# Where GpSimd pauses between indirect transfers: a pause after every second one in four more places of a graph-network kernel

## The reference

```
x = x + _L0_gnn_ref(_layernorm(x), edge_index, W, a)        # weighted sum of neighbours' rows, summed by source
x = x + _L0_ffn_ref(_layernorm(x)[None], ...)               # 32 experts, one per node, hidden size 64
x = x + _L1_gnn_ref(_layernorm(x), edge_attr_8, edge_attr_4, ...)  # messages from edge attributes
x = x + _L1_ffn_ref(_layernorm(x)[None], ...)               # 6 experts, two per node, three layers of 256
x = x + _L2_gnn_ref(_layernorm(x), src, dst, ...)           # attention over edges, then a dense FFN
x = x + _L2_ffn_ref(_layernorm(x)[None], ...)               # dense mixture
x = x + _L3_gnn_ref(_layernorm(x), W, att, src, dst)        # attention over edges
x = x + _L3_ffn_ref(_layernorm(x)[None], ...)               # 8 experts, two per node
```

```
h = x @ W
e = exp(-leaky_relu((h @ a1)[src] + (h @ a2)[dst]))
h' = segment_sum(e * h[dst], src) / segment_sum(e, src)
```

## Time and profile before

| | us |
|---|---|
| median of 3 runs | 5369.42 (5359.68 to 5380.3) |
| the profiled execution | 5363.28 |
| its span in the profile | 5361.2 |
| first loop, first to last gather | 302.4 to 1030.1 |
| first FFN's slots, last SRT scatter to last result | 1217.7 to 1455.6 |
| two-expert slots | 2468 to 2648 and 5153 to 5322 |

### The profile page before, as it was taken

The page is one execution under the profiler, slowest core; times in us unless marked ns, Lnnn a source line. Parts: engine busy times, 40 slices in busy tenths (PEclk is TensorE's granted clock), DMA queues, the critical chain, the costliest instruction groups (busy, mean ns, idle before and its releaser), DMA issues.

```text
span 5361.2 us, 75037 instructions
## 1 busy us (share of the span) xinstructions
PE 3835.8 (72%) x19152; PEld 2523.5 (47%) x19152; DVE 3230.3 (60%) x8314; ACT 2680.6 (50%) x8902; POOL 2678.8 (50%) x3199
## 2 busy tenths in 40 slices
PE   6868888631529999987666776668999935556665
PEld 2336565431314444456545555545655524444454
DVE  9955666350337998876567788753333435555743
ACT  6835666420217888863336666653233325555522
POOL 4655555647357776704427777731000056666244
PEclk9978988755758999998888888889999967677778
DMA  3023322321313333422345555530000033333334
GB/s 121 21 73 82 80 78 78 59 51 36 106 46 89 90 89 86 87 41 93 105 129 160 160 161 161 159 85 0 12 12 16 6 93 86 86 84 85 34 118 131
DMA packets 278825, 441.41 MB, mean 82 GB/s; under 512 B 114083, under 2 KB 192781, under 8 KB 278157
## 3 DMA queue, kind: packets, MB, share of 16 engines
q0 software_dynamic: 124624, 331.70, 24.1%
q1 hardware_dynamic: 147230, 98.37, 6.4%
q10 hardware_dynamic: 6560, 6.55, 0.4%
HBM read 368.84 MB, written 67.60 MB: 81 GB/s over the span
## 4 chain that ended last, share of the span: by engine, by line
PE 40%; DVE 18%; another core or an unknown queue 12%; issue 12%; ACT 6%; POOL 6%; DMA 4%; DVEq 2%; ACTq 0%; POOLq 0%; SPq 0%
PE PB L3159 6%; PE PB L2012 5%; PE PB L2542 3%; PE PB L3143 3%; POOL bigt L2660 3%; PE PB L735 3%; PE PB L1092 2%; DVE bigt L714 2%; PE PB L1587 2%; ACT XNT L2626 2%; PE PB L1575 2%; PE PB L2022 2%; DMA bigt<-KVTAB,DO 2%; POOL X L2660 1%
## 5 line engine op out<-in xcount | busy, mean ns | idle before, releaser
L2542 PE MATMUL PB<-XNT 128*128 128x260 f32 x1760 | 598.5, 474 | 115.8 <-issue 46.0
L2660 POOL DMA_INDIRECT bigt<-ZTAB,DO x440 | 456.5, 1037 | 274.8 <-issue 120.8
L1036 POOL DMA_INDIRECT bigt<-HTAB,bigt x440 | 420.9, 957 | 314.1 <-ACT bigt L726 154.4
L1984 POOL DMA_INDIRECT bigt<-YTAB,bigt x440 | 473.5, 1076 | 140.3 <-issue 128.1
L366 POOL DMA_INDIRECT RECS<-bigt x391 | 388.4, 993 | 241.7 <-DVE bigt L714 96.0
L735 PE MATMUL PB<-bigt 128*128 128x440 f16 x1564 | 395.5, 382 | 89.5 <-issue 63.0
L2542 PEld LDWEIGHTS PB<-XNT 128*128 128x128 f32 x1760 | 366.1, 230 | 193.0 <-issue 66.4
L2626 ACT ACTIVATE XNT<-bigt 128x65 f32<-128x65 f32 x1768 | 446.2, 336 | 0.0
L726 ACT ACTIVATE bigt<-bigt 128x128 f16<-128x128 f16 x1214 | 374.3, 389 | 78.6 <-DVE bigt L699 41.6
L2012 PE MATMUL PB<-bigt 128*128 128x512 f32 x880 | 405.3, 603 | 3.0 <-DVE bigt L2200 3.0
L2660 POOL DMA_INDIRECT bigt<-KVTAB,DO x296 | 294.9, 996 | 214.5 <-DMA KVTAB<-bigt 83.5
(11 more groups left out here) (491 smaller groups left out, 9549.0 us busy)
## 6 DMA issues: line engine op xcount, KB each, us to landing
bigt<-YTAB,bigt POOLq DMA_INDIRECT x552
bigt<-SRT SPq DMA_DIRECT2D x56, 128.0 KB
OUTS<-bigt SPq DMA_DIRECT2D x56, 128.0 KB
SRT<-bigt SPq DMA_DIRECT2D x11, 640.0 KB, 9.9
bigt<-HTAB,bigt POOLq DMA_INDIRECT x440
bigt<-ZTAB,DO POOLq DMA_INDIRECT x440
KVTAB<-bigt SPq DMA_DIRECT2D x25, 258.0 KB
YTAB<-bigt SPq DMA_DIRECT2D x10, 640.0 KB, 9.6
```

The costliest lines, as they stand in the source:

```text
L1036: e.indirect_dma_start(out=Gt[:, g % GB, j, :], out_offset=None, in_=HTAB, in_offset=bass.IndirectOffsetOnAxis(ap=SO[:, g * G + j:g * G + ...
L1984: e.indirect_dma_start(out=Gt[:, g % GB, j, :], out_offset=None, in_=YTAB, in_offset=bass.IndirectOffsetOnAxis(ap=SO[:, g * G + j:g * G + ...
L2542: m = e.matmul(self.PV[n % len(self.PV)], self.OH[:, g % 2, j, :], self.msg[:, g % 2, j, :], start=(k == 0), stop=(k == self.H - 1))
L2660: e.indirect_dma_start(out=dst[:, j, :], out_offset=None, in_=table, in_offset=bass.IndirectOffsetOnAxis(ap=DO[:, g * G + j:g * G + j + 1] ...
```

## The change

- In the first loop the extra wait of a group's second pair (for `lanes_made` or `oht_kept`) is gone, and `rest(e)` stands after each pair of gathers.
- `attr_scatters` with n > 1 rests after every second scatter in place of every fourth. The calls with n = 1 (the first sort) have none, as before.
- The second batch of scatters in the first FFN has 30 in place of 36. The six are issued later: 65 in place of 59 are left for the second graph layer.
- The 25 SRT scatters rest after every second one.
- In the two-expert FFNs GpSimd rests once in each round of slots.

The calls of `rest` go from 279 to 698, that is 558 memsets to 1396. No instruction of another engine changes.

```
-                if (c - first) % 4 == 3:
+                if n > 1 and c % 2:
                     rest(e)
...
                         if g >= GB and j % 2 == 0:
                             e.wait_ge(*half(weighed, 2 * (g - GB) + j // 2))
-                            c = MOVES * (g - FIRST) + 1
-                            if j == 2 and 0 <= c < EC:
-                                e.wait_ge(*sort_d.lanes_made.at(sort_d.act_cols.index(c)))
-                            elif j == 2 and g - 3 < SG:
-                                e.wait_ge(*oht_kept.at(g - 3))
                         elif g >= 2 and j == 0:
                             e.wait_ge(*onehot.at(g - 2))
                         e.indirect_dma_start(
...
                         ).then_inc(gathered.sem(g), 16)
+                        if j % 2:
+                            rest(e)
...
                             ).then_inc(fetched.sem(s), 16)
+                        rest(e)
                     return
                 attr_scatters(e, 30)
                 e.wait_ge(*begun.last)
-                attr_scatters(e, 36)
+                attr_scatters(e, 30)
...
                         in_=xs[:, t, :], in_offset=None).then_inc(rows_out.sem, 16)
+                    if t % 2:
+                        rest(e)
                 attr_scatters(e, 116)
```

More of the change, by code:

```diff
@@ L354, in attr_scatters @@
         def attr_scatters(e, n):
-            first = recs_next[0]
-            for c in range(first, min(EC, first + n)):
+            for c in range(recs_next[0], min(EC, recs_next[0] + n)):
                 piece, k = divmod(c, PIECE)
@@ L1028, in pool_edges @@
                             e.wait_ge(*half(weighed, 2 * (g - GB) + j // 2))
[L1029 to L1033, removed]
                         elif g >= 2 and j == 0:
```

## The result

| | us |
|---|---|
| the changed kernel, median of 4 runs | 5230.01 (5220.94 to 5244.43) |
| the kernel before, same chip, 4 runs | 5371.21 (5359.68 to 5380.3) |
| ratio | 0.9741, 95% interval 0.9711 to 0.977 |
| the profiled execution; its span | 5244.43; 5242.7 |

The change makes the kernel faster by 141 us on this chip, where the forecast said 189 (5180); the time lies inside the range. A *stop* is here, as in the prediction, a stretch of a few us in which an engine waits for a signal that nothing in the profile claims ("remote"). The experiments add something that no profile of one chip could tell: **of the six chips that the experiments went to, two run the kernel before in 4850 us, the stops that the change removes are not there, and every set of its pauses that was run there costs time (the scatters' 34 us, the first loop's 139, the two-expert slots' 59 by the profiles).**

A forecast was written before the change was run, and what follows sets the result against it. Engines stand waiting for signals that come late while GpSimd issues indirect transfers without real pauses (12% unclaimed). Terms -63 -32 -10 +5 -68 -10 -11 sum to -189: 5363.3 to 5174, or 5180 by median; 8-in-10 range 5140 to 5345.

The forecast's parts named there:

- First loop, -63: First loop's 110 groups: stops go, GpSimd sets the pace, 727.7 us become 665; bounds -77 and 0.
- I take 0.45, by the nearer form: First loop: price of a pause in us, taken near the scatters' +0.43 and not the third graph layer's +0.74.
- Tail, -32: After the first loop's gathers, 61.9 us: without stops about 30 us; bounds 0 and -34.
- Routing -10, SRT +5: Routing, 67.8 us: stops go, -10; then 12 pauses among the SRT scatters stand on the path, +5.
- Slots, -68: First FFN's slots: all 56 results done within 172 us of scatters by twos, GpSimd's 76.9 us idle time gone.
- Second layer's start, -10: Second graph layer's start: 65 scatters by twos and a landing take 99.5 us against 109.6; bounds +15 and -12.
- Two-expert slots, -11: Second and last two-expert FFN: -8 and -3, pauses hidden while slots take over 3.0 us; bounds +10 and -25.
- The rest, 0: Second layer's loop, third and fourth graph layers, dense FFNs: same instructions, no change.
- The rival of half relief among scatters (5276): Pauses by two help only half as well among scatters as among gathers: sum -93, 5276; chance of half relief 0.26.
- The 5392 and 5452 of the slower rivals: Pauses that relieve nothing in loop or scatters, +29: 5392; dearer pauses, +89: 5452; chance of slower 0.15.
- GpSimd's pace takes the place of the stops, dearer than they are: First loop: pauses hold engines up instead of stops; at 0.95 us each the loop is +34, total 5452; slower 0.15.
- The rival of another cause: Stops come from something like code fetching, not GpSimd; loop unchanged: 5392 (slower 0.15) or 5375 (no change 0.07).

The follow-up runs named there:

- loop_alone_2: Kernel before with pauses after each pair of first-loop gathers and ScalarE's extra waits gone, on a chip with stops: 5306 us against 5367, ratio 0.989.
- no_slot_rest: Changed kernel without the pauses in the two-expert slots, on a chip with stops: 5209 us, ratio 0.9699 to the kernel before (5368).
- after_again: Changed kernel run once more, unchanged, on a chip with stops: 5226 us, ratio 0.974 to the kernel before (5368).
- waits_alone: Kernel before with ScalarE's extra first-loop waits gone and no pause put in, on a chip without stops: 4849 us against 4850, ratio 0.9997.
- loop_alone: Kernel before with pauses after each pair of first-loop gathers and ScalarE's extra waits gone, on a chip without stops: 4989 us against 4850, ratio 1.028.

## Why the prediction came out as it did

The mechanism was right, for the kind of chip it was made on: pauses remove stops of all engines, and GpSimd takes their place. By its steps:

- **First loop, -63: -23.** The step that failed is the price of a pause. "I take 0.45, by the nearer form" chose the scatters' row; it is 3.17 - 2.51 = 0.66 in place of 0.45 (the KVTAB pairs' 0.74, set aside, were nearer), and 220 x 0.21 = 46 us are the miss. The rest held: GpSimd is the bound, remote waits and waits for ScalarE are gone, and of the 2% allowed for loss 1% came (704.9 us in place of 220 x 3.17 = 697).
- **Tail, -32: -46.** 61.9 us became 15.8, as the engines end the loop less far behind (41 of the 46 by the loop's own pauses, in loop_alone_2). Both together: -95 forecast, -68 measured.
- **Routing -10, SRT +5:** first SRT scatter from 1185.8 to 1102.8, -83, so -15 beyond the -68, and the SRT scatters took 36.9 us in place of 31.6, +5.
- **Slots, -68: -65** (first SRT scatter to OUTS 272.6, then 213.2, which is -59 with the +5 in it). Pairs of scatters start 2.97 us apart, as 2 x 1.27 + 0.43 had it. The largest and least sure term was right, for the reason given: all 56 results are there before the scatters end.
- **Second layer's start, -10: -10** (from the last OUTS gather's end 109.9 before and 99.9 after, for 65 scatters with their pauses and a landing).
- **Two-expert slots, -11: about +11.** The sign failed: from the last FFN's first gather to the span's end it is 222.1 us before (5361.2 - 5139.1), 233.3 after, 221.8 in no_slot_rest. "Each pause is hidden as long as slots take over 3.0 us" used the short price; at 3.2 us a round GpSimd is the bound of the last FFN, and in the second FFN the pauses brought nothing (171.5 and 171.9).
- **The rest, 0:** the terms down to the second layer's start make -152 at SyncE's first read of RECS. The profiled execution, the slowest of four, then gave back 23 us in unchanged stages (5139.1 to 5009.4 is -129.7 at the last FFN's first gather). In after_again it is 4987.4 there, -151.7: nothing was given back. So I take it for one execution's spread and not for an effect of the change, and the median's -141 is then -152 and +11.

Of the signs that the prediction named, the waits of L1036 for ScalarE's L726 and of DVE L714 on "remote" are gone, all 56 results come before the scatters end, and a pause in the loop cost under 0.8 us; the loop's last gather came at 1007 us and not near 965, by the price of the pause. SyncE's first read came 152 us earlier and not 190: of the forecast's terms only -178 lie ahead of it, and the loop's miss of 40 was in part made good by the tail.

The rival of half relief among scatters (5276) isn't what happened: VectorE keeps 48.9 us of stops in the slots' stretch, but the slots are through before GpSimd. The 5392 and 5452 of the slower rivals are counted from the profiled execution and 5276 from the median, 6 us apart.

Of the other rivals, "GpSimd's pace takes the place of the stops, dearer than they are" is what happens on the two chips without stops, at a pause of 0.67 us and not 0.95: whether it decides hangs not on the pause's price alone but on what the stops cost on the chip. The rival of another cause, such as fetched code, doesn't hold as it was put: pauses of GpSimd end the stops while no less code is fetched (173 and 247 packets in the instruction queues after, 173 and 238 before), and nearly the same program fetches as much on a chip without stops (173 and 239 in waits_alone). What the forecast never weighed is that the stops could be the chip's and not the program's.

Not settled: what in a chip delays the signals. The Trainium skill ("DMA: Bandwidth & Descriptors", section "Why a DMA increments its semaphore by 16 and not by 1") has all sixteen engines write to the semaphore of a transfer that GpSimd issues, whatever its shape, so by that rule both kinds of chip got the same stream, and the sixteen writes by themselves can't be the cause. No run here varies them. The Trainium skill ("Advanced Engine Details and Errata", section "DMA Bandwidth Details") puts an increment at about one cycle. No trace here resolves a cycle; on the two chips without stops nothing speaks against it, as no wait is on "remote", and on the others it leaves VectorE's 3.51 us between two of its own instructions unexplained.

## What to carry to other kernels

A wait that a profile puts down to nothing it knows, on all engines at once, can belong to the chip it ran on: run the unchanged kernel on several chips before tuning it away, since the cure has its price on every chip (here -2.6% on one kind, an estimated +5% on the other). Price a pause, or any filler, by the row with the same instruction behind it, and compare the issuing engine's whole round with the round of the stage: in the last FFN a round of 3.20 us with the pause, where the stage went at 3.03 without it, was enough to make the filler the bound.

## What the runs showed of the hardware

- The same program takes 4847 to 4850 us on two chips, and 5309 to 5371 us in the other five sets of runs, the seven to thirteen runs of a set of experiments within 0.6% of each other. A gather takes GpSimd 957 ns on both kinds; what differs is when waiting engines go on while GpSimd issues indirect transfers. The granted clock of TensorE differs too, 0.87 against 0.84 over the span, but goes with the loop's length: 0.94 in the 558 us of waits_alone, and in the 705 us with pauses 0.91 on a chip without stops (loop_alone) as on one with them (the changed kernel).
- In the first loop, without stops, a waited scratch write between two pairs of gathers costs 0.17 us, two cost 0.67 ((704.1 - 557.4) / 219), two that aren't waited for 0.38 ((640.7 - 557.4) / 219).
- Gathers in a row without any pause are no harm where a chip has no stops: the loop of waits_alone ran at 557.4 / 439 = 1.27 us a gather, its bare pace (0.96 and 0.30).
